# A graph-network kernel: the second attention pass finishes each block itself

## The reference

```python
alpha = jnp.einsum('ehc,ehc->eh', q[dst], k[src]) / np.sqrt(ch)
m = jax.ops.segment_max(alpha, dst, num_segments=n)
ea = jnp.exp(alpha - jax.lax.stop_gradient(m)[dst])
denom = jax.ops.segment_sum(ea, dst, num_segments=n)
attn = ea / (denom[dst] + EPS)
out = jax.ops.segment_sum(attn[:, :, None] * v[src], dst, num_segments=n)
return out.reshape(n, heads * ch) + (x @ Ws + bs)
```

## Time and profile before

| | |
|---|---|
| median of three runs | 4392.54 us |
| time of the profiled execution | 4394.14 us |
| its span | 4392.3 us |
| VectorE busy in the span | 3062.9 us (70%) |
| GpSimd busy in the span | 2731.0 us (62%) |
| TensorE matrix work busy in the span | 2837.4 us (65%) |
| gathers of e21 | 858 = 26 x 33, mean 990 ns |
| phase e21, from its first VectorE instruction to its last copy | 2448.6 to 3594.5 us |
| phase f21, its VectorE work | 3595.6 to 3605.6 us |

### The profile page before, as it was taken

How to read it: one execution, slowest core, us unless ns; L and a number is a source line. 1 busy time by engine, 2 the same in 40 slices (tenths; PEclk the granted TensorE clock), 3 DMA queues, 4 the chain that set the end, 5 groups by cost and what they waited for, 6 DMA issues and landing times. The chain is left out here.

```text
span 4392.3 us, 62771 instructions
## 1 busy us (share of the span) xinstructions
PE 2837.4 (65%) x19910; PEld 2520.7 (57%) x19911; DVE 3062.9 (70%) x7097; ACT 1079.8 (25%) x1379; POOL 2731.0 (62%) x2657
## 2 busy tenths in 40 slices
PE   3677676757635656565557466666665657996688
PEld 2566566656635645555556355555555547885566
DVE  4767776777766666676665577777777777997445
ACT  2222232222212222222221212222222223452000
POOL 3777777777557777777771577777777732553000
PEclk7566666656567776767779677776777768998799
DMA  3222222222234445544551233333333314451453
GB/s 71 59 60 60 59 60 59 59 59 60 45 86 126 128 135 140 136 124 132 138 147 50 78 103 102 103 102 103 102 101 102 102 51 98 115 119 32 159 131 90
DMA packets 163300, 415.60 MB, mean 95 GB/s; under 512 B 61300, under 2 KB 88272, under 8 KB 156841
## 3 DMA queue, kind: packets, MB, share of 16 engines
q0 software_dynamic: 95296, 224.30, 19.4%
q1 hardware_dynamic: 64404, 187.52, 16.2%
q10 hardware_dynamic: 3432, 1.61, 0.1%
HBM read 345.77 MB, written 67.48 MB: 94 GB/s over the span
## 5 line engine op out<-in xcount | busy, mean ns | idle before, releaser
L560 POOL DMA_INDIRECT e21G<-table,e21src x858 | 849.4, 990 | 392.0 <-issue 256.8
L560 POOL DMA_INDIRECT e0G<-table,e0src x858 | 858.6, 1001 | 312.1 <-issue 255.4
L1533 POOL DMA_INDIRECT t1G<-table,t1idx x806 | 792.6, 983 | 311.5 <-issue 241.4
L1606 PE MATMUL t1psW<-t1CO,t1G 128*128 128x192 f32 x1612 | 431.6, 430 | 304.4 <-issue 289.1
L1606 PEld LDWEIGHTS t1psW<-t1CO,t1G 128*128 128x128 f32 x1612 | 367.7, 257 | 311.8 <-issue 295.0
L2272 POOL TENSOR_TENSOR e22Z<-e22Z,e22C 121x847 f32<-121x847 f32 (+1 forms) x104 | 200.2, 1956 | 259.6 <-ACT e22Z L2264 259.6
L593 PE MATMUL e0psQ<-Q,e0OT 121*128 x1716 | 307.3, 318 | 39.7 <-issue 35.2
L593 PEld LDWEIGHTS e0psQ<-Q,e0OT 121*128 121x128 f32 x1716 | 305.1, 282 | 45.2 <-issue 45.2
L600 PE MATMUL e21psQ<-Q,e21OT 121*128 x1716 | 246.5, 294 | 102.0 <-DVE e21G L844 62.3
L600 PEld LDWEIGHTS e21psQ<-Q,e21OT 121*128 121x128 f32 x1716 | 214.6, 199 | 134.6 <-DVE e21G L844 89.3
L1845 DVE TENSOR_TENSOR t1AT<-t1AT,t1psW 128x192 f32 x186 | 65.1, 350 | 313.4 <-PE t1psW L1606 312.9
(11 more groups left out here) (445 smaller groups left out, 5766.7 us busy)
## 6 DMA issues: line engine op xcount, KB each, us to landing
e22C<-counts SPq DMA_DIRECT2D x26, 1487.0 KB
llC<-planes SPq DMA_DIRECT2D x52, 743.5 KB
Q<-in_type_p SPq DMA_DIRECT2D x62, 416.0 KB
counts<-X SPq DMA_DIRECT2D x13, 1487.0 KB
planes<-SKIP SPq DMA_DIRECT2D x26, 743.5 KB
counts<-RES SPq DMA_DIRECT2D x13, 1487.0 KB
e0G<-table,e0src POOLq DMA_INDIRECT x858
e21G<-table,e21src POOLq DMA_INDIRECT x858
```

Source lines behind the costliest of these rows:

```text
L560: nc.gpsimd.indirect_dma_start(out=G[:, u, t, 0:width], out_offset=None, in_=table, in_offset=bass.IndirectOffsetOnAxis(ap=src[:, u, t:t + ...
L1533: nc.gpsimd.indirect_dma_start(out=G[:, q % 2, t, :], out_offset=None, in_=table, in_offset=bass.IndirectOffsetOnAxis(ap=idx[:, q * GT + t ...
L1606: mmi = nc.tensor.matmul(psW[:, k % 2, 0:WIN * NBAS], G[:, q % 2, t, :], CO[:, k % 2, i].rearrange("p b w -> p (b w)"), start=(i == 0), st ...
```

## The change

In the pass (when it is not `gat`), the copy of line 929 is replaced by four VectorE instructions with drains between them: 1e-16 is added to the block's 8 sums of weights into a new tile `den`, `den` is inverted, the 128 sums are multiplied with it into `acc`, and `acc` and the block's skip rows are added into the block's row of RES. The call of `transformer_finish` for f21 is taken out. RES then holds the 128 features alone, which is all that p22 reads.

```diff
@@ -154,7 +154,6 @@
         attention_pass(g, "e21", tab[256], 256, 8, False)
-        transformer_finish(g, "f21", 8, last=False)
         with ExitStack() as ctx:
@@ -482,6 +481,7 @@
         one = sb("one", [BN, 1])
+        den = sb("den", [BN, H])
@@ -926,7 +926,16 @@
                     if gat:
                         V.tensor_copy(two[:, u, :], ST[:])
                     else:
-                        V.tensor_copy(RES[:, bass.ds(blk, 1), 0:NC].rearrange("p a f -> p (a f)"), ST[:])
+
+                        row = RES[:, bass.ds(blk, 1), 0:D].rearrange("p a f -> p (a f)")
+                        V.tensor_scalar(den[:], ST[:, D:D + H], 1e-16, None, ALU.add)
+                        dve.drain()
+                        V.reciprocal(den[:], den[:])
+                        dve.drain()
+                        V.tensor_tensor(acc[:, 0:D].rearrange("p (h c) -> p h c", h=H), ST[:, 0:D].rearrange("p (h c) -> p h c", h=H),
+                                        bc(den[:].unsqueeze(2), [BN, H, C]), ALU.mult)
+                        dve.drain()
+                        V.tensor_tensor(row, acc[:, 0:D], g["SKIP"][:, bass.ds(blk, 1), :].rearrange("p a f -> p (a f)"), ALU.add)
```

## The result

The changed kernel took 4396.45 us (median of 20 runs, 4388.81 to 4404.24), the kernel before 4390.27 us (20 runs, 4385.20 to 4395.69). The ratio is 1.0015, with a 95% interval of 1.0008 to 1.0022. The kernel is slower by some 6 us. That is within the 0.2% that the prediction called no change, but outside the predicted range and on the other side of before. The profiled execution took 4395.84 us, with a span of 4393.8 us.

What follows compares the result with a forecast made beforehand. The prediction took GpSimd's gathers to set the pass's pace, with VectorE barely keeping up. Its terms, -10.73 + 0.92 + 1.4 = -8.4 us, gave a median of 4384.1 us, range 4379 to 4393 us.

Steps and rivals of the forecast that it cites:

- The stage, -10.73 us: Between pass and p22: removing f21 saves 10.73 us of VectorE work and one meeting of the engines.
- rival E: Start of p22: something fetched in f21's shadow makes it slow, up to 3.4 us come back, 4387.5 us; chance 0.10.
- The price of a step, 0.88 us: Pass, end of each step: the added instructions and drains lengthen VectorE's chain by 0.88 us.
- The last step's 0.92: End of the pass: behind the last copy nothing hides the last step's added 0.92 us.
- The slack, 1.65 us a trip: Pass loop: GpSimd's gathers set 85.30 us a trip; VectorE's chain alone takes 83.65, leaving 1.65 us for two steps.
- B: Pass: the gathers keep the pace and there is no surplus, -9.8 us, 4382.7 us; chance 0.22.
- Rival D: Pass: the added two-input operations hold up at most one gather a step, 12.0 us, so +2.2 us, 4394.7 us; chance 0.04.
- The surplus of 0.11 us a trip: Pass: VectorE's chain becomes 85.41 us against 85.30 a trip, adding up to 1.4 us over 12.5 trips.
- Rival C: Pass: more of TensorE's sums at the lower clock, trip 86.19 us, 11.1 us in all, total +1.3 us; chance 0.12.
- Behind the pass, 0 us: After p22's start, dense attention included: the prediction gave it no term and took it as unmoved.
- S: Pass: VectorE's chain clearly sets the pace, trip 86.93 us, total +10.9 us, 4403.4 us; chance 0.05.
- L: Pass loop, 12 instructions longer: no longer stays loaded, a slow entry in each of 13 trips, some 54 us; chance 0.01.

Runs made afterwards that it cites:

- x1: Kernel before with the f21 stage taken out and the copy to RES kept, so division and skip rows are left out: 4381.64 us against 4388.60, ratio 0.9980.
- x4: Changed kernel with the sum of weights plus 1e-16 formed beside the merge, one dependent instruction fewer in the chain: 4389.42 us against 4392.77 before, ratio 0.9994.
- x5: Kernel before with three additions of 8 words, each with a drain, ahead of the copy to RES: 4399.85 us against 4392.77, ratio 1.0014.
- x13 to x15: Changed kernel with two, five and eight VectorE memsets at the end of the pass: 4389.82, 4391.46 and 4401.68 us against 4390.53 before.
- x2: Changed kernel with a stage of the same instructions, working on scratch, kept behind the pass: 4404.45 us against 4388.60 before, ratio 1.0040.
- x3: Changed kernel with the first step's division in each trip moved into the second step's waits for TensorE: 4380.99 us against 4388.60 before, ratio 0.9981.
- x6: Kernel before with four additions of 8 words, each with a drain, ahead of the copy to RES: 4407.16 us against 4392.77, ratio 1.0036.
- x8: Changed kernel with 24 and 8 unread matrix instructions filling two TensorE gaps ahead of each step's sums: 4386.99 us against 4389.54 before, ratio 0.9991.

## Why the prediction was wrong

- **The stage, -10.73 us:** right. x1 shows 10.7 us; entry and weights' wait are unchanged, so rival E fell.
- **The price of a step, 0.88 us:** measured 0.93 (1.10 us where 1.06 was forecast: 0.21 us and not 0.17 ahead of the last instruction; the remaining 0.01 us is the rounding from 0.89 to 0.88). The last step's 0.92 came out as 0.97: 15.1 - 10.73 + 0.97 = 5.3 us, against 5.4 measured.
- **The slack, 1.65 us a trip, and GpSimd's pace:** right in the main. The waits for rows went to 0.3 us and the gathers' pace did not move, so rivals B and D fell. The slack was read a little too small: before the change, the products of line 844 in step 13 lie 1.38 us apart where nothing is waited for and 2.96 us across the wait (3047.92 to 3050.88), 1.58 us more and not 1.50, and over steps 2 to 25 such delays make 1.79 us a trip.
- **Rival D:** it was weighed with a rule of the Trainium skill (SBUF — State Buffer, "SBUF: two separate sides"), that a VectorE operation with two SBUF inputs and a GpSimd operation that reads SBUF block each other for a whole instruction. The trace shows no such loss at this size: the gathers beside lines 935 and 938 took 0.95 us.
- **The surplus of 0.11 us a trip: this is the step that failed.** With 0.93 us it would have been 83.65 + 1.86 - 85.30 = 0.21 us, 2.6 us in all, and with the slack of 1.79 us less still. Measured were 0.85 us, and 9.6 us. What the sum put at nothing is the 0.74 us a trip by which TensorE's sums grew: with it and the slack of 1.79 us a trip comes to 85.30 - 1.79 + 1.86 + 0.74 = 86.11 us, against 86.15 measured. The sum kept one long and one short step of sums in each trip, as in the trace of before. That still held in x4 and, from step 5 on, in x5, at +0.85 and +0.86 us a step, and no longer in the changed kernel at +0.93: the edge lies between, and why it lies there stays open. The price that was assumed, 0.88, falls into this gap, so it can't be said whether the forecast would have come true at its own price. Rival C had the mechanism and almost the number (trip 86.19 against 86.15 measured, in the pass +11.1 against +9.6, and total +1.3 us against -0.1 for pass and stage together), and got 0.12. Its form was not quite as put: not both steps of a trip at the long value, but a course of eight steps through short, long and longer ones, whose mean of 11.23 us happens to lie at the long value of before (11.2 to 11.3), so its number is in part luck. The argument held against it was that nothing showed two long steps in a row, and the trace that it was read from has the shorter chain, in which they do not occur.
- **Behind the pass, 0 us: the second term put at nothing without a reason.** Measured were +6.4 us in the dense attention. The prediction took everything behind p22 as unmoved. x13 to x15 show that a few small instructions ahead of this part move its time by up to 10 us; x5, with three additions in the pass of before and 389.3 us, and x2, with the changed pass and 382.4 us, that it is not tied to the one pass or the other. That the moment of the start also lies behind the 6 us between the two kernels is a reading that was not shown, and neither was why the changed kernel's dense attention is long in three of three profiles.
- **The other rivals:** S needed a surplus of 1.46 us a trip and L would have cost some 54 us; neither came.
- **One sign could not tell:** the last write to RES was to end at 3596 to 3597 us, past 3605 under C. It ended at 3599.43, but the pass's first copy alone comes anywhere from 2516.5 to 2525.9 us in the same kernel, so a time counted from the span's start decides nothing here.

In sum: pass and stage together gave -0.1 us where -8.4 was forecast, and the dense attention +6.4.

## What to carry to other kernels

A chain that gets longer than the slack of its loop can cost much more than the surplus: here 0.85 us a trip where the sum gave 0.1 to 0.2, because the time that another engine takes for its part had moved too. So a loop's slack should not be spent to its end on paper. Before work is moved into a loop from behind it, see which waits of the receiving chain it can be hidden in, as x3 did, rather than count on the average slack. When the expected gain is some microseconds, compare several profiles stage by stage: a stage that the edit does not touch may move by as much.

## What the runs showed of the hardware that was not expected

- The same 66 matrix instructions took 9.79 to 11.37 us within one pass, by how much of them fell at the lower clock (granted 0.85 to 0.73).
- The changed kernel's chain is 0.08 us a step longer than x4's, and its pass 10.2 us longer; x6's is 0.2 us a step longer than x5's, and its pass 10.9 us longer.
- In x4 VectorE waited for no gathered row, and its trips still kept the 85.3 us of the kernel before.
- The dense attention, 2782 matrix instructions in each run, took 379.8 to 393.3 us in the profiles, with a granted clock of 0.95 to 0.92, and two to eight memsets ahead of it were enough to change it.
- Matrix instructions that compute nothing of use made a kernel faster: x8 was 2.6 us below the kernel before, and the changed kernel that it fills 6.2 us above it.
- The addition of line 938, with two operands placed by a register, started 0.21 us behind the end of the instruction before it, the copy of line 929, with one, 0.17 us. The next step's first product, behind a register load from SBUF, started 0.83 us behind the start of either.
